# First cross attention: heads written out, values made by key for two heads, the last 26 keys in one product, scores cut at bank borders

## What is computed

```python
xn = layernorm(ctx_1024, gamma_media, beta_media)       # 154 rows
ln = layernorm(layernorm(x), gamma_lat, beta_lat)       # 1024 rows
q = ln @ Wq + bq
kv = concat([xn, ln], axis=1) @ Wkv + bkv               # 1178 rows
k, v = split(kv, 2)
sim = (q * DH ** -0.5) @ k.T          # per head, 1024 x 1178
out = softmax(sim) @ v
x = x + tanh(g_xattn[0]) * (out @ Wo + bo)
```

## Time and profile before

| what | value |
|---|---|
| median of 3 runs | 3512.09 us (3511.55 to 3512.71) |
| the profiled execution, its time | 3516.88 us |
| its span | 3514.8 us |
| mean granted clock of TensorE | 0.974 |
| PE busy | 3196.8 us, 91% |
| DVE, ACT, POOL busy | 69%, 48%, 18% |
| where the first attention ends | shortly before 1780 us |

### The profile page before, as it was taken

One profiled execution on the slowest core, in us unless ns is written; L12 is line 12 of the kernel. 1 busy time (PEld: TensorE's weight loads), 2 busy tenths in 40 slices (PEclk: granted clock), 3 DMA queues, 4 the chain that ended last, 5 costly groups with the idle time before them and its releaser, 6 DMA issues. The chain is left out here.

```text
span 3514.8 us, 63123 instructions
## 1 busy us (share of the span) xinstructions
PE 3196.8 (91%) x21044; PEld 2927.6 (83%) x21044; DVE 2413.2 (69%) x4474; ACT 1694.3 (48%) x3134; POOL 648.4 (18%) x738
## 2 busy tenths in 40 slices
PE   4999899998999989999969999999999979999688
PEld 3999889998899989999957788898989868888467
DVE  5666666666666676666666677777787766666787
ACT  3555555555555555555533322222222246666587
POOL 3111121111211212111011121111111023322220
PEclk9999999999999999999989999999999979999799
DMA  3000000000000000000020032323323200000001
GB/s 86 8 12 14 7 14 7 12 14 7 14 7 12 14 7 13 13 6 1 1 54 5 6 90 89 107 91 113 92 87 93 81 20 1 0 0 0 25 15 35
DMA packets 120564, 111.76 MB, mean 32 GB/s; under 512 B 39952, under 2 KB 86345, under 8 KB 120393
## 3 DMA queue, kind: packets, MB, share of 16 engines
q1 hardware_dynamic: 120392, 109.57, 10.7%
HBM read 104.28 MB, written 5.24 MB: 31 GB/s over the span
## 5 line engine op out<-in xcount | busy, mean ns | idle before, releaser
L369 ACT ACTIVATE x_pth<-x_ps 128x512 fp32r<-128x512 f32 (+1 forms) x768 | 375.3, 527 | 266.1 <-PE x_ps L574 265.7
L462 DVE TENSOR_TENSOR x_ptl<-x_ps,x_pth 128x512 fp32r<-128x512 f32 (+1 forms) x768 | 436.0, 595 | 76.8 <-ACT x_pth L369 68.5
L849 ACT ACTIVATE moe_sil<-moe_ps,moe_b 128x512 f32<-128x512 f32 x256 | 176.3, 689 | 564.0 <-PE moe_ps L1003 558.2
L374 ACT ACTIVATE x_p<-x_p,x_nmx 128x1178 f32<-128x1178 f32 x256 | 327.7, 1280 | 248.7 <-DVE x_p L479 248.7
L574 PE MATMUL x_ps<-ident,x_p 128*128 128x128 f32 x2560 | 371.6, 276 | 43.0 <-DVE x_ptl L462 43.0
L574 PEld LDWEIGHTS x_ps<-ident,x_p 128*128 128x128 f32 x2560 | 301.3, 141 | 92.9 <-DVE x_ptl L462 73.8
L596 PE MATMUL x_ps<-x_pth,x_vh 128*128 128x256 f32 x1280 | 375.3, 293 | 1.6 <-DVE xres L498 1.6
L1026 PE MATMUL moe_ps<-moe_w2z,moe_gh 128*128 128x256 f32 (+1 forms) x1280 | 370.5, 289 | 4.3 <-DVE moe_gl L966 4.3
L596 PE MATMUL x_ps<-x_ptl,x_vh 128*128 128x256 f32 x1280 | 365.0, 285 | 0.0
L596 PE MATMUL x_ps<-x_pth,x_vl 128*128 128x256 f32 x1280 | 364.8, 285 | 0.0
L1026 PE MATMUL moe_ps<-moe_w2z,moe_gl 128*128 128x256 f32 x1280 | 362.4, 283 | 0.0
(11 more groups left out here) (358 smaller groups left out, 7994.4 us busy)
## 6 DMA issues: line engine op xcount, KB each, us to landing
moe_gate<-moe_cw_rows SPq DMA_DIRECT2D x512, 128.0 KB, 2.9
x_wraw<-in_L_xattn_Wkv_dram SPq DMA_DIRECT2D x64, 128.0 KB, 2.3
xres<-in_x_dram SPq DMA_DIRECT2D x4, 1024.0 KB, 7.4
x_wraw<-in_L_xattn_Wq_dram SPq DMA_DIRECT2D x32, 128.0 KB, 2.3
x_wraw<-in_L_xattn_Wo_dram SPq DMA_DIRECT2D x32, 128.0 KB, 2.0
moe_w1r<-in_L_ffn_w_dram SPq DMA_DIRECT2D x8, 512.0 KB, 5.9
moe_w2r<-in_L_ffn_w_dram SPq DMA_DIRECT2D x4, 1024.0 KB, 9.7
out_dram<-xres SPq DMA_DIRECT2D x8, 512.0 KB, 2.9
```

The lines of the kernel that those rows point to most:

```text
L369: act.activation(pth[:, (v // 2) % 2, lo:hi, (v % 2) * P:(v % 2 + 1) * P], ps[:, TURN + (v + g) % 2, 0:(hi - lo) * P].rearrange("p (n t) - ...
L374: act.activation(p[:, w % 4, DUP:DUP + R_KV], p[:, w % 4, DUP:DUP + R_KV], ACT.Exp, bias=nmx[:, w % 2:w % 2 + 1], scale=-1.0, accum_out=su ...
L462: dve.tensor_tensor(ptl[dst], ps[:, TURN + (v + g) % 2, 0:(hi - lo) * P].rearrange("p (n t) -> p n t", t=P), pth[dst].bitcast(F32), ALU.su ...
L849: act.activation(dst[:, q % 2, :], ps[:, HID + q % 2, :], ACT.Silu, bias=bias).then_inc(silu_done, 1)
```

## The change

- **Loops.** Heads are written out: 64 steps are a batch's body, in a loop of three passes, with 8 steps ahead and 64 behind. Jobs come from a table per head (`MAKES`), at most one at the start of a step (`begin`) and one after the scores (`middle`).
- **Values.** They are made with keys on partitions: the stationary operand is a block of 128 keys of the input, the moving one is Wv of two heads (256 columns), ten blocks for two heads. The "t" jobs and `vf` are gone. The value bias leaves the values; multiplied by Wo (8 products at the start) it joins the output bias.
- **The last 26 keys.** They are laid three times, at partitions 0, 32 and 64, as (high, low, high) of the weights against (high, high, low) of the values, so one product of 96 rows replaces three. POOL copies the two repeats into `p` in every step (`tail_set`).
- **Scores and keys** are cut into 512, 512 and 154 columns; DVE reads 1178 columns in a row.
- **Order on PE in a step:** begin job, groups 1 and 2, scores, middle job, projection (even steps), group 3, values (blocks 0 to 4 on even, 5 to 9 on odd steps). The projection has bank 7 to itself; after the first batch's entry all jobs use bank 6 alone. The projection comes six, its sum seven steps after the tile.
- **Weights** are loaded and split one kind at a time by a fixed list (`SPLITS`).
- **Normalising** of the next batch lies at the ends of steps 54, 55 and 56, the output bias is added in steps 16 and 17.
- **Start.** Statistics of batch 0 and the context come first; those of the other 24 tiles after the first head's jobs, ahead of step 0 on DVE.

The diff, cut to its core:

```diff
-SN = 2 * -(-R_KV // 6)
-DUP = 3 * SN - R_KV
+R_FULL = R_KV // P
+R_TAIL = R_KV - R_FULL * P
+R_SET = 32
...
-        scores = ps[:, 0:3, 0:SN]
-        TURN, PV, JOB = 3, 5, 6
+        scores = ps[:, 0:3, :].rearrange("p b c -> p (b c)")
+        TURN, PV, JOB, YB = 3, 5, 6, 7
...
+        CUT = ((0, CH), (CH, 2 * CH), (2 * CH, R_KV))
+        PART = ((0, 5), (5, R_BLK))
...
+        def even(n):
+            v, j = vals(n // 2, 4, R_BLK), kq(n + 1)
+            return [v[0:2], v[2:4], v[4:6], j[0:1], j[1:2], j[2:3], j[3:4], j[4:5]]
+
+        def odd(n):
+            v, j = vals((n + 1) // 2, 0, 4), kq(n + 1)
+            return [j[0:1], j[1:2], j[2:3], j[3:4], j[4:5], v[0:1], v[1:3], v[3:4]]
...
+            for w in range(LOOP):
+                step(0, w, False, True)
             with eng.Fori(0, BATCH - 1) as b:
+                for w in range(LOOP, STEPS):
+                    step(b, w, True, True)
+                for w in range(LOOP):
+                    step(b + 1, w, True, True)
+            for w in range(LOOP, STEPS + LOOP):
+                step(BATCH - 1, w, True, False)
...
+                pool.wait_ge(exp_done, STEPS * b + w + 1)
+                at = R_FULL * P
+                for r in (1, 2):
+                    last = pool.tensor_copy(p[:, w % 4, at + r * R_SET:at + r * R_SET + R_TAIL], p[:, w % 4, at:at + R_TAIL])
+                last.then_inc(tail_set, 1)
...
+                if hi > mid:
+                    r = slice(R_SET, 2 * R_SET)
+                    dst = turn_dst(pth, x, mid, hi)[r, :, :]
+                    last = dve.tensor_tensor(dst, turn_src(x, g)[r, mid - lo:hi - lo, :], dst.bitcast(F32), ALU.subtract)
...
+                last = m - (2 if early else 1)
+                if last >= 0 and ORDER[last][0] == "v":
+                    pe.wait_ge(v_low, NVALS * b + VALS_AT[last])
+                elif last >= 0:
+                    pe.wait_ge(job_full, NFULL * b + FULL_AT[last])
...
+                    s, rows = 0, v_rows(lo)
+                    for k in range(KT):
+                        for x, w in ((kvh, wvh), (kvh, wvl), (kvl, wvh)):
+                            last = pe.matmul(out[rows, :], x[:, k, lo * P:lo * P + rows.stop], w[:, k, :], start=(s == 0), stop=(s == 5))
...
-                for n in range(R_BLK):
-                    for i, (v, x) in enumerate(((vh, pth), (vh, ptl), (vl, pth))):
+                for c in range(*PART[part]):
+                    if c < R_FULL:
+                        for i, (v, x) in enumerate(((vh, pth), (vh, ptl), (vl, pth))):
+                            pe.matmul(out, v[:, slot(n), c, :], x[:, u % 2, c, :], start=(c == 0 and i == 0), stop=False)
+                    else:
+                        rows = slice(0, 3 * R_SET)
+                        pe.matmul(out, vh[rows, slot(n), c, :], pth[rows, u % 2, c, :], start=False, stop=True).then_inc(pv_done, 1)
...
+                x = behind(w, TURN_LAG, 1, before)
+                if x is not None:
+                    turn(b, x, 0)
+                    turn(b, x, 1)
+                if w < STEPS:
+                    score(b, w)
+                for j in middle:
+                    job(*j)
+                u = behind(w, O_LAG, 2, before)
+                if u is not None:
+                    project(b, u)
+                if x is not None:
+                    turn(b, x, 2)
```

More of the change, by code:

```diff
@@ L132, in resample_stage @@
[L132 to L137, removed]
+        none = sb("none", [P, 2])
@@ L156, in resample_stage @@
[L156 to L171, removed]
@@ L328, in _, with root_of @@
+            split(0, "v", 0)
+            no_split()
+            split(0, "k", 0)
+            split(0, "q", 0)
+            for m in range(len(ENTRY_ALL)):
+                if ORDER[m][0] != "v":
+                    low(0, m)
+            split(0, "k", 1)
+            split(0, "o", 0)
+            split(0, "q", 1)
+            steps(pool, step)
         @block.scalar
         def _(act):
+            def root_of(rows, n):
+                act.wait_ge(stats, n)
+                act.activation(root[:, rows], var[:, rows], ACT.Sqrt).then_inc(rooted, 1)
@@ L387, in _ @@
+            for m in range(len(ENTRY_ALL)):
+                job(0, m, True)
+            act.wait_ge(job_low, FULL_AT[len(ENTRY_ALL) - 1] + JLOW0)
+            act.activation(bvb, bias[:, 2, :].unsqueeze(2).broadcast_to([P, R_HEADS, P]), ACT.Copy).then_inc(bv_spread, 1)
+            root_of(late, 3)
+            root_of(late, 4)
+            act.activation(tg[:, :], tg[:, :], ACT.Tanh).then_inc(tanhed, 1)
+            steps(act, step)
         @block.vector
@@ L389, in _ @@
             own = Chain(dve, dve_own)
[L390 to L392 removed]
+            dve.sem_inc(s_read, READ0)
+            dve.sem_inc(lo_done, LOW0)
+            dve.sem_inc(o_split, SPLIT0)
+            dve.sem_inc(y_added, ADD0)
             own.link(dve.memset(mv[:, :, :], 1.0))
[L394 to L397 removed]
@@ new lines, in step @@
+            def step(b, w, before, after):
+                begin, middle = planned(b, w, after)
+                for j in begin:
+                    job(*j)
+                u = behind(w, O_LAG, 2, before)
+                if u is not None:
+                    dve.wait_ge(o_high, UNITS * b + u + 1)
+                    dve.tensor_tensor(ol[:, :], ps[:, PV, 0:2 * P], oh[:, :].bitcast(F32), ALU.subtract).then_inc(o_split, 1)
+                x = behind(w, TURN_LAG, 1, before)
+                if x is not None:
+                    low(b, x, 0)
+                    low(b, x, 1)
```

793 lines of the change are left out of this document (405 added, 388 removed).

## The result

| what | before | after |
|---|---|---|
| median of 4 runs each, side by side | 3512.40 us (3511.55 to 3516.72) | 3383.59 us (3380.23 to 3385.82) |
| ratio, 95% interval | | 0.9630 (0.9613 to 0.9647) |
| the profiled execution, its time | 3516.88 us | 3380.23 us |
| its span | 3514.8 us | 3378.5 us |
| mean granted clock of TensorE | 0.974 | 0.976 |

The change takes 128.8 us off; 111 were forecast, and 3383.6 lies in the range of 3350 to 3460.

The account below looks back on a forecast made before the run. TensorE was taken to bound the first attention, half the span. Products -22, `vf` wait -54, low parts -28, written-out heads -4 and start -3 sum to -111 us, giving 3401 against the median; 80% range 3350 to 3460.

Parts of the forecast that it names:

- Products: PE's products per head: fewer for values and last keys, dearer cuts of scores and keys; together -22.2 us.
- s: Price of one 154-column product on PE, taken as 0.110 us like a 128-column transpose, between 0.076 and 0.120.
- (c) and (d): Scores and keys cut 512, 512, 154 on PE: +25.3 us for scores, +6.3 us for keys.
- Rival 2: The 154-column products cost only what they stream, 0.076 to 0.084 us; time 3368 to 3376 us; chance 0.16.
- The wait for `vf`: PE's transposes of the values no longer exist to wait for ACT's copy; 54 us go.
- that for the low parts: PE's weight transposes wait less for DVE: crossings 23 us, half the other waits 17, new ones 12; net -28.
- the crossings give 23 us: At three batch crossings PE's standing, restart and slow products go: 3 x (6.2 + 0.2 + 1.4) us.
- New waits: DVE's normalising in three steps per crossing and bias in two steps per batch; 12 us charged in all.
- One bank for jobs: Each job waits for the previous one's drain; covered by other PE work, cost 0, otherwise about 1 us each.
- Heads written out: Three passes of a longer loop replace 16 of an inner one; 6.1 us of issue waits mostly go, -4.
- Start: Only batch 0 measured first; first score pass about 66 instead of 68.45; -3 us, between -8 and +4.
- Rival 1: DVE or ACT take over what waits gave: 3442 us if half returns, 3480 if nearly all; chance 0.20.

Follow-up runs that it names:

- experiments 2: Changed kernel with scores and keys cut into three stretches of 394 columns again: 3359.13 us, ratio 0.9567.
- 10: Changed kernel with scores and keys in three cuts of 394 columns and the 24 late statistics put between the entry jobs: 3349.59 us, ratio 0.9537.
- run 11: The changed kernel again with nothing edited, on another chip: 3389.94 us, ratio 0.9649.
- experiment 3: Changed kernel with the product of the last 26 keys issued three times instead of once: 3409.22 us, ratio 0.9707.
- experiment 1: Kernel before, with the value jobs a step earlier, apart from the transposes of the values: 3488.40 us, ratio 0.9937.
- Experiments 5: Changed kernel with the third group of transposes right behind the scores again, as before the change: 3386.19 us, ratio 0.9645.
- experiment 6: Changed kernel with all 28 products of a unit on the even step instead of split over two: 3500.03 us, ratio 0.9961.
- 7: Changed kernel with the third group right behind the scores and all 28 products on the even step: 3562.86 us, ratio 1.0136.
- experiment 4: Changed kernel with the 24 late statistics of x moved between the first head's entry jobs: 3372.67 us, ratio 0.9600.
- experiment 8: Changed kernel with both jobs of a step at its start, back to back in the one bank: 3514.36 us, ratio 1.0002.

## Why the prediction was right, and where its terms were off

The mechanism and the size came out: faster, by 128.8 where 111 were forecast. By its terms:

- **Products**, forecast -22.2, found about -25. The argument from the transposes held: s was taken as 0.110 and is 0.107 over whole heads. Terms (c) and (d), 31.6 us dearer together, measure 30.0 and 31.3 (experiments 2, and 10 against 11), and the product of the last keys costs its 0.12 (experiment 3). The 81 ns for 128 columns of the Trainium skill (TensorE: Matmul & The Clock Gate, Back-to-back issue gap) are lower than what these pairs of load and product show on average. Rival 2 (0.076 to 0.084) is out by price, though the time, 3383.6, is nearer to its 3376 than to 3401; that nearness comes from the waits.
- **The wait for `vf`, -54, and that for the low parts, -28.** With the issue waits (-4) the forecast has -86, found are about -101, and this is where the forecast and the result part. Both waits are gone (0 and 1.8). "I let half of them go" was the term that was mis-sized: 39.2 of 41.0 went, and with the other 17 us it is 86 + 17 = 103. That they are one debt (experiment 1) matters for what each is worth alone, not where both go. In "the crossings give 23 us" the 1.4 us of slow products per crossing didn't go; they moved behind the wait for `z`, against the text's "no stretch at 1.2 GHz". Two readings there are off without touching the sum: the block of the earlier trace rows normalises two pairs of tiles, not four, and the pace of 52.70 us a head is low, since the passes over the scores give 53.14, so that 3.9 us a head were waits and not 3.4.
- **What removed the low-part wait** was put down to work between the groups and to the split in equal breath. Experiments 5 to 7 say that either removes it nearly whole. But the split does more, which the forecast didn't have: without it the time is 116 us longer, and not by this wait but by two that the kernel before didn't show, the second group for the low part of the tail and the single bank of jobs, since on odd steps the 13 products cover DVE's pass over the scores. The forecast priced the split as part of a 17 us credit.
- **New waits**, forecast 12 us for normalising and bias: 11.8 us at L633. Right in size; they stand at the entry jobs, which wait for `z`. Three crossings hold six of them, 4 us each time, and with the slow products behind and 0.5 us for `kvl` a crossing still costs some 6 us.
- **One bank for jobs**, forecast 0 with a margin of 0.5 us: 0 in after, and 1.5 us a pair of values where the cover is taken. The price "about 1 us" was too low by a third, since it counted the drain and not the queue in front of it on ACT and DVE.
- **Heads written out, -4.** Not found: issue waits of 4.0 and 7.6 us in two executions, against 6.1 before, in two places as before. It is no term at all.
- **Start, -3**: found -1.9, with 7 us by the trace, 10.9 by the medians, left lying in the wait of 8.24 us and the statistics around it (experiment 4).
- **Rival 1** didn't happen: DVE is busy 73.89 of 100 us, and no wait for it in a plain step is left. Experiments 6 and 7 show what it would have looked like.
- **The rest of the span** is 8.3 us shorter from the last score pass on (1744.1 instead of 1752.4), 6 to 7 of it outside the stage; the change doesn't touch that part, and the profiled execution of before was 4.5 us over its median. In the profiled executions of run 11 and of experiments 2, 3, 4 and 10 the same part took 1743.6 to 1748.8 us.

## What to carry to other kernels

Price products by the distance of two starts: summed over a head they gave the time of the changed kernel to 2%, and edits of PE's own work (experiments 2 and 3) moved the 255 steps by 30.0 of 31.6 and 26.2 of 30.7 us. Take the distance up to where the rhythm is again that of the wide products, or the price of a small one is read too low. Waits of one engine for another don't add: remove one and see whether its neighbour takes over, and look at the shortest step, not at an engine's mean share of idle time: work in program order behind a long pass is covered only by what the other engine has in that very step. Before giving up a buffer, price its loss with what stands in the queues of the engines that drain it, not with their two instructions alone.

## What the runs showed of the hardware

A product of 154 columns behind one of 512 starts its successor after 0.07 us, less than the 0.110 of a transpose of 128 columns; the next two take 0.11 and 0.12, and a product of 256 columns behind them 0.16 instead of 0.12. What the first saves the one behind gives back, so that three cost 0.34 us. That it is the load, which a wide product ahead would hide, fits the rows but wasn't measured by itself. The return of a loop of 64 steps cost PE about 2.0 us twice in one execution of the changed kernel, and 3.6 and 4.0 in another. And a wait as the profile lists it is 0.16 us short of the distance that is lost: 0.88 for 0.72 (experiment 6), 1.71 - 0.12 = 1.59 for 1.43 (experiment 8).
